# Square sums of the up weights by TensorE in place of ScalarE

## Reference

```python
kv = ctx @ W_k.T + b_k                      # ctx [4, 512, 128]
out = einsum('bij,bjd->bid', layernorm(x), kv)
sim = einsum('bid,bjd->bij', out, kv) * 512 ** -0.5
sim = layernorm(sim) * ln_gamma + ln_beta
x = x + softmax(sim)
n = layernorm(x)
scores = einsum('btd,ed->bte', n, Wg)       # 8 experts, the best 2 per token
w = softmax of the best 2 scores, on their experts, else 0
h = silu(n @ W1[e].T) * (n @ W2[e].T)       # W1, W2 [8, 352, 512]
y = sum over e of w[e] * (h @ W3[e].T)      # W3 [8, 512, 352]
return x + y
```

## Time and profile before

| | us |
|---|---|
| median of 3 runs | 399.23 (399.21 to 400.86) |
| profiled execution | 399.87 |
| its span in the profile | 397.8 |
| around the span | 2.1 |

### The profile page before, as it was taken

One profiled execution on the slowest core, in us unless ns is written; L12 is line 12 of the kernel. 1 busy time (PEld: TensorE's weight loads), 2 busy tenths in 40 slices (PEclk: granted clock), 3 DMA queues, 4 the chain that ended last, 5 costly groups with the idle time before them and its releaser, 6 DMA issues.

```text
span 397.8 us, 8115 instructions
## 1 busy us (share of the span) xinstructions
PE 362.7 (91%) x2277; PEld 239.1 (60%) x2277; DVE 253.2 (64%) x677; ACT 251.1 (63%) x433; POOL 156.7 (39%) x189
## 2 busy tenths in 40 slices
PE   6869799889797699999999999999999999999981
PEld 5445567567784356566666666666666666666640
DVE  1336566987978895763466757667676766757660
ACT  2168787857650698994475666656666575666650
POOL 2114564555831204225544353433435344352321
PEclk9989989996855799999999999999999999999997
DMA  7998799996840214425353545545354453544424
GB/s 224 418 416 322 251 339 356 398 326 230 250 158 2 80 29 64 97 53 87 77 94 67 105 66 98 78 84 95 70 104 68 93 86 75 107 63 100 77 32 53
DMA packets 21833, 57.60 MB, mean 145 GB/s; under 512 B 4832, under 2 KB 4960, under 8 KB 20256
## 3 DMA queue, kind: packets, MB, share of 16 engines
q0 software_dynamic: 8736, 20.53, 29.1%
q1 hardware_dynamic: 11040, 21.62, 15.3%
q10 hardware_dynamic: 2016, 14.94, 10.3%
HBM read 38.17 MB, written 18.91 MB: 143 GB/s over the span
## 4 chain that ended last, share of the span: by engine, by line
PE 63%; DVE 4%; issue 3%; DMA 3%; POOL 1%; ACT 1%; POOLq 1%; ACTq 0%; DVEq 0%
PE bank L1214 35%; PE bank L1235 15%; PE bank L1225 5%; PE bank L1205 4%; PE bank L1257 3%; DMA out<-kvj_s,sidx 1%; DMA ng_s<-n_table,gidx 1%; PE bank L1122 1%; DMA n_table<-wrow 1%; DVE Wp L793 1%; PE bank L1106 1%; DVE stage L817 0%; PE bank L1049 0%; POOLq L73 0%; POOL rstd L418 0%
## 5 line engine op out<-in xcount | busy, mean ns | idle before, releaser
L1214 PE MATMUL bank<-Wp,kvg_s 128*128 x480 | 79.7, 317 | 2.6 <-DVE kvg_s L949 2.4
L1214 PE MATMUL bank<-Wp,kv_s 128*128 x456 | 74.3, 313 | 0.2
L943 DVE SCALAR_TENSOR_TENSOR stage<-W,w3sc,stage 128x512 f16<-128x512 f16 x93 | 66.9, 748 | 7.5 <-ACT stage L615 7.5
L1235 PE MATMUL bank<-stage,n_s 128*128 128x512 f16 (+1 forms) x279 | 65.3, 379 | 1.5 <-issue 1.5
L1214 PEld LDWEIGHTS bank<-Wp,kvg_s 128*128 128x128 f16 x480 | 47.3, 99 | 31.0 <-issue 5.9
L615 ACT ACTIVATE stage<-W,w3sc 128x512 f16 x93 | 63.4, 719 | 0.0
L475 POOL DMA_INDIRECT out<-oT_s,sidx x20 | 31.8, 1589 | 76.8 <-ACT oT_s L646 69.4
L1214 PEld LDWEIGHTS bank<-Wp,kv_s 128*128 128x128 f16 x456 | 44.4, 98 | 26.2 <-issue 3.3
L475 POOL DMA_INDIRECT out<-kvj_s,sidx x19 | 30.1, 1585 | 66.8 <-ACT kvj_s L646 64.3
L459 POOL DMA_INDIRECT ng_s<-n_table,gidx x39 | 39.0, 1000 | 32.1 <-DVE gidx L912 13.8
L970 DVE TENSOR_TENSOR n_s<-bank,n_s 128x384 f16<-128x384 f32 x31 | 17.3, 558 | 51.8 <-ACT n_s L628 51.8
(11 more groups left out here) (188 smaller groups left out, 564.7 us busy)
## 6 DMA issues: line engine op xcount, KB each, us to landing
Wp<-in_w ACTq DMA_DIRECT2D x6, 1408.0 KB, 10.3
W<-in_w ACTq DMA_DIRECT2D x8, 768.0 KB, 5.8
stage<-in_xT SPq DMA_DIRECT2D x4, 1024.0 KB, 7.3
W<-in_x SPq DMA_DIRECT2D x12, 256.0 KB, 7.4
out<-W SPq DMA_DIRECT2D x12, 256.0 KB, 8.4
Wp<-in_w SPq DMA_DIRECT2D x2, 1408.0 KB, 13.4
n_table<-n_s SPq DMA_DIRECT2D x8, 256.0 KB, 3.6
n_table<-x_s SPq DMA_DIRECT2D x8, 256.0 KB, 4.1
```

Source lines behind the costliest of these rows:

```text
L943: eng.scalar_tensor_tensor(w3p[r][:, W3N + c * D:W3N + (c + 1) * D], W3[:, bass.ds(e * W3N + c * D, D)], w3sc[:, bass.ds(e, 1)], w3p[r][:, ...
L1214: mm = eng.matmul(bank[2 * which + r][:, 0:H], n_, w_, start=(c == 0 and k == 0), stop=(c == DC - 1 and k == 2))
L1235: mm = eng.matmul(ybank(t)[:, :], h_, w_, start=(c == 0 and k == 0), stop=(c == HC - 1 and k == 2))
```

## The change

The squares leave ScalarE. TensorE takes the upper 16 bits of each float32 word as a bfloat16 (a view with a step of two elements, 4 bytes), and multiplies each 128x128 block of expert k's weight by itself, transposed: 22 blocks, added up in 128 columns of bank 5. On the diagonal of that product stand the square sums of the 128 column positions. VectorE multiplies it by the identity and sums each row into `wsq` (`diagonal`). The sum over partitions, as before, is over all 128 of them. Only the upper halves of the words are used, so the scale is of slightly truncated weights; the scale is divided out again.

The products take the place of the warm matmuls in slots 0 to 13: all 22 in slots 0 and 1, then 11 a slot. Slot 14 has neither, 15 and 16 keep the warm run. The products of expert k wait for its load and for VectorE's reading of expert k-1's diagonal (`s_wq`). The chain to the scales starts one slot later (15 in place of 14) and so do its steps; on GpSimd the power now stands behind the norm of its slot and not ahead. `table(0)` goes from slot 13 to 14. The issue of the loads is in the same slots.

```diff
@@ -56,6 +56,7 @@
 GROUPS = ((0, 4), (4, 4), (8, 4), (12, 3), (15, 1))
 WARM_GATHER = 12
 WARM_SLOT = 12
+GRAM_SLOTS = ((0,), (1,), (2, 3), (4, 5), (6, 7), (8, 9), (10, 11), (12, 13))
 WARM_START = 48
 NSCALE = 2.0 ** 10
 WSCALE = 2.0 ** 15
@@ -90,7 +91,7 @@
 
         xT_s = stage[:, 0:DC * N]
         ctx_s = stage[:, DC * N:DC * N + T]
-        wjunk = Wp[:, 0:WH].bitcast(BF16)
+        upper = [Wp[:, (e + 1) * 2 * W12N:(e + 2) * 2 * W12N].bitcast(BF16).rearrange("p (n t) -> p n t", t=2)[:, :, 1] for e in range(E)]
         x_s = [W3[:, g * D:(g + 1) * D] if g < G - TPB else stage[:, DC * N + (g - G + TPB) * D:DC * N + (g - G + TPB + 1) * D]
                for g in range(G)]
         wk_s = sb("wk_s", [P, C])
...
@@ -225,8 +227,8 @@
         s_w = [sem(f"s_wl{i}") for i in range(E)]
         s_w3 = [sem(f"s_w3_{i}") for i in range(E)]
 
-        s_wq, s_wqp, s_wsum, s_wmax, s_wrs, s_wsc, s_wrec, s_winv = [
-            sem(n) for n in ("s_wq", "s_wqp", "s_wsum", "s_wmax", "s_wrs", "s_wsc", "s_wrec", "s_winv")]
+        s_wg, s_wq, s_wqp, s_wmax, s_wrs, s_wsc, s_wrec, s_winv = [
+            sem(n) for n in ("s_wg", "s_wq", "s_wqp", "s_wmax", "s_wrs", "s_wsc", "s_wrec", "s_winv")]
         s_hi, s_lo = sem("s_hi"), sem("s_lo")
         s_w3q, s_w3qp, s_w3s, s_w3r, s_w3sc, s_w3rec, s_yinv, s_yt = [
             sem(n) for n in ("s_w3q", "s_w3qp", "s_w3s", "s_w3r", "s_w3sc", "s_w3rec", "s_yinv", "s_yt")]
@@ -431,12 +433,12 @@
                 if real(bn_):
                     scale(bn_, in_)
                 n = TPB * (b + 1) + i - (TPB - 1)
-                if n == 2 * E - 1:
-                    eng.wait_ge(s_wmax, 1)
-                    eng.tensor_tensor(wrs[:, :], wsum[:, :], half[:, 0:1].to_broadcast([P, E]), ALU.pow).then_inc(s_wrs, 1)
                 b1, i1 = lag(b, i, 1)
                 if real(b1):
                     norm(b1, i1)
+                if n == 2 * E:
+                    eng.wait_ge(s_wmax, 1)
+                    eng.tensor_tensor(wrs[:, :], wsum[:, :], half[:, 0:1].to_broadcast([P, E]), ALU.pow).then_inc(s_wrs, 1)
                 if i == 1 and real(b + 1):
                     gamma_keys(b + 1)
                 if n == 17:
@@ -511,7 +513,6 @@
             def slot(b, i):
                 n = TPB * (b + 1) + i - (TPB - 1)
                 weight_loads(n)
-                weights(n)
                 b3, i3 = lag(b, i, 3)
                 if real(b3):
                     g = g_of(b3, i3)
@@ -561,12 +562,6 @@
                 cols = bass.ds(b * TPB, TPB)
                 eng.activation(edl[:, cols], dlt[:, cols], ACT.Exp).then_inc(s_ed, 1)
 
-            def squares(k, h):
-                eng.wait_ge(s_w[k], 16)
-                wait(eng, s_wq, 2 * k + h)
-                eng.activation(wjunk, wst[k][:, h * WH:(h + 1) * WH], ACT.Square,
-                               accum_out=wsq[:, k, h:h + 1]).then_inc(s_wq, 1)
-
             def w12_high(k, h):
 
                 if k >= E:
@@ -589,17 +584,10 @@
                         eng.wait_ge(s_n, (e + 1) * W3N // D)
                     eng.dma_start(W3[:, e * W3N:(e + 1) * W3N], w3[e]).then_inc(s_w3[e], 16)
 
-            def weights(n):
-
-                if n // 2 + 1 < E:
-                    squares(n // 2 + 1, n % 2)
-
             eng.wait_ge(s_key, 16 * 3)
             kv_evac(0)
             kvj_evac(0)
             o_evac(0)
-            squares(0, 0)
-            squares(0, 1)
             batches(slot)
             router_exp(B - 1)
 
@@ -768,9 +756,13 @@
 
             def weight_sums():
                 eng.wait_ge(s_wqp, 1)
-                eng.tensor_reduce(wsum[:, :], bank[7][:, E:3 * E].rearrange("p (e h) -> p e h", h=2), AX.X, ALU.add).then_inc(s_wsum, 1)
-                eng.wait_ge(s_wsum, 1)
-                eng.tensor_tensor(wsum[:, :], wsum[:, :], guard[:, :], ALU.max).then_inc(s_wmax, 1)
+                eng.tensor_tensor(wsum[:, :], bank[7][:, E:2 * E], guard[:, :], ALU.max).then_inc(s_wmax, 1)
+
+            def diagonal(k):
+
+                eng.wait_ge(s_wg, k + 1)
+                eng.tensor_tensor_reduce(diag[:, :], bank[5][:, P:2 * P], ident[:, :], 1.0, 0.0, ALU.mult, ALU.add,
+                                         wsq[:, k:k + 1]).then_inc(s_wq, 1)
 
             def weight_scale():
 
@@ -805,6 +797,10 @@
                     hold(eng, 4, (s_T, g + 1), (s_E, g - 1))
                     eng.tensor_tensor_reduce(L_s[:, k, :], L_s[:, k, :], beta_s[:, :], 1.0, 3.0e38, ALU.add, ALU.min,
                                              lmin[:, k:k + 1]).then_inc(s_L, 1)
+                n = TPB * (b + 1) + i - (TPB - 1)
+                for k in range(E):
+                    if n == GRAM_SLOTS[k][-1] + 1:
+                        diagonal(k)
                 b1, i1 = lag(b, i, 1)
                 if real(b1):
 
@@ -822,8 +818,7 @@
                     square_in(b + 1)
                 if i == 2 and real(b + 1):
                     gram_copy(b + 1)
-                n = TPB * (b + 1) + i - (TPB - 1)
-                if n == 2 * E:
+                if n == 2 * E + 1:
                     weight_scale()
                 if i == 0 and real(b - 2):
                     router_weights(b - 2)
@@ -853,7 +848,7 @@
                     scale_in(bn_, in_)
                 if i == 3 and real(b + 2):
                     centre_keys(b + 2)
-                if n == 2 * E - 2:
+                if n == 2 * E - 1:
                     weight_sums()
                 if i == 0 and 1 < b < B:
                     places(b - 2)
@@ -1108,8 +1103,18 @@
 
             def weight_norms(n):
                 wait(eng, s_sc, n - 4)
-                eng.wait_ge(s_wq, 2 * E)
-                eng.matmul(bank[7][:, E:3 * E], ones[:, :], wsq[:, :, :].rearrange("p e h -> p (e h)"), start=True, stop=True).then_inc(s_wqp, 1)
+                eng.wait_ge(s_wq, E)
+                eng.matmul(bank[7][:, E:2 * E], ones[:, :], wsq[:, :], start=True, stop=True).then_inc(s_wqp, 1)
+
+            def weight_gram(k, first, last):
+
+                eng.wait_ge(s_w[k], 16)
+                wait(eng, s_wq, k)
+                for c in range(first, last):
+                    w_ = upper[k][:, c * P:(c + 1) * P]
+                    mm = eng.matmul(bank[5][:, P:2 * P], w_, w_, start=(c == 0), stop=(c == W12N // P - 1))
+                if last == W12N // P:
+                    mm.then_inc(s_wg, 1)
 
             def router(b, i):
                 g = g_of(b, i)
@@ -1166,7 +1171,12 @@
                     keys(b + 2)
                 if i == 0 and real(b + 1):
                     turn_keys(b + 1)
-                warm(ones16[:, :], WARM_SLOT)
+                if n > GRAM_SLOTS[E - 1][-1] + 1:
+                    warm(ones16[:, :], WARM_SLOT)
+                for k, slots in enumerate(GRAM_SLOTS):
+                    if n in slots:
+                        h, part = slots.index(n), W12N // P // len(slots)
+                        weight_gram(k, h * part, (h + 1) * part)
                 turn_n(*lag(b, i, 2))
                 if i == 1 and real(b + 1):
                     gram(b + 1)
@@ -1174,7 +1184,8 @@
                 if i == 2 and real(b + 1):
                     gram_outs(b + 1)
                     sims(ba, ia)
-                if n == 13:
+                if n == 14:
+                    eng.wait_ge(s_wq, E)
                     table(0)
             eng.wait_ge(s_const, NCONST)
             warm(ones16[:, :], WARM_START)
```

More of the change, by code:

```diff
@@ L129, in build @@
         guard = sb("guard", [P, E])
-        wsq = sb("wsq", [P, E, 2])
+        wsq = sb("wsq", [P, E])
+        diag = sb("diag", [P, P])
         wsum = sb("wsum", [P, E])
```

## The result

| | before | changed kernel |
|---|---|---|
| median of the runs, us | 399.86 (399.21 to 400.86, 4 runs) | 403.94 (402.52 to 404.42, 4 runs) |
| profiled execution, us | 399.87 | 402.52 |
| its span, us | 397.8 | 399.9 |
| ratio to before (95% interval) | | 1.0087 (1.0062 to 1.0112) |

The change made the kernel slower by about 4 us, where no change was forecast, and the median lies beyond the upper end of the range (402.2). The profiled execution is the fastest of its four: its trace shows a little less of the loss than the median has. The ratios leave out runs in a slower state, one of `a4_three` (482.15 us) and two of `b2_no_squares_loads` (402.75 and 403.21); the medians have them in.

The account below looks back on a forecast made before the run. With the expert stage fixed, the time hung on when the first gathered rows reach TensorE. Terms -2.4 -0.9 +0.9 +1.1 +1.2 = -0.1 us took 399.23 to 399.1 us; terms' ends 397.2 to 401.2, range with rivals 396.0 to 402.2.

Parts of the forecast that it names:

- The hand-over in slot 10: Slot 10: TensorE's products wait for VectorE's diagonal behind the minimum, making outs(3) late; +1.1 us.
- Part 1: Slots 0 to 3: squares off ScalarE let the scaling start sooner; 2.4 us gained, from 0.7 to 3.1.
- the unfavourable end: Start, slots 0 to 3: earlier third-weight load shares the engines, xT lands at 32.1, gain only 0.7 us.
- rival D: Start: ScalarE's freed time only issues loads earlier, which hold up inputs; gain 0.7 us, 400.8 us, chance 0.11.
- Part 2: Slots 4 to 16: squares are hidden by waits and gain nothing, except 0.9 us in slot 13.
- The 0.9 us of slot 13: Slot 13: a square delays the router's exp, for which VectorE idles; removing it gains 0.9 us.
- Rival A: Slots 5, 6, 7, 10, 11: ScalarE paces, so removed squares pass through by half; 3.7 us faster, 395.5 us, chance 0.24.
- Part 3: TensorE, slots 0 to 14: products replace warm matmuls, 4-byte step costs nothing; taken as 0, bound 0.6 us per eleven.
- Rival B: TensorE, slots 0, 1, 2, 7, 10: strided products run at half rate; 3.0 us slower, 402.1 us, chance 0.11.
- Part 4: VectorE's diagonals cost 0.9 us in slots 8, 12, 14; TensorE's wait for one in slot 10 costs 1.1 us.
- Rival C: Slots 1, 2, 6 too: TensorE waits for the diagonal, VectorE for products; 401.6 us, chance 0.14.
- Part 5: Slots 16 and 17: pow behind GpSimd's norm delays VectorE's weight_scale and router copy; +1.2 us, from 0.5 to 2.0.

Follow-up runs that it names:

- a4_three: Changed kernel with third and fourth loads held, diagonals of experts 2 to 7 at the slot's head, pow ahead of the norm: 398.77 us, 0.9968.
- b2_no_squares_loads: Kernel before without ScalarE's squares, nothing in their place, third and fourth up-weight loads held until the first two landed: 398.42 us, 0.9947.
- the last two kernels: Changed kernel with only slot 10's diagonal at its slot's head, 400.80 us, and with only those of experts 2, 3, 4, 6, 7 there, 403.96 us.
- a2_diag_first: Changed kernel with VectorE's diagonals of experts 2 to 7 at the head of their slots: 401.08 us, 1.0022.
- a6_two: Changed kernel with two edits, third and fourth loads held and diagonals of experts 2 to 7 at the slot's head: 399.17 us, 0.9964.
- a0_after: The changed kernel itself, unaltered, in a second set of five runs: 403.32 us, 1.0070.

## Why the prediction was wrong, step by step

Two terms of the sum failed. The start was put at -2.4 us on the ground that alpha of tile 3 would be last at slot 4; xT was, and the lead there was 1.3 us. The hand-over in slot 10 was put at +1.1 us, the delay of one arrival; TensorE's rows there have 3.4 us, because the wait came together with a lower clock. The late norms, +1.2, were put too high and hid some of it.

**Part 1, the start: the step that failed first.** The mechanism of both sides was written down and the wrong side was taken. The scaling of tile 0 came at 22.59 (22.3 forecast). But xT, and not alpha of tile 3, was last at slot 4: it landed at 33.03 (16.97 + 16.06), even later than the 32.1 of the unfavourable end, and the lead at tile 3 was 1.3 us, nearer to the 0.7 of rival D than to the 2.4 taken. My estimate had the second and the third weight share evenly from 19.3 on and counted only the rows' mean rate. I also gave the late xT no price beyond its lateness. In the changed kernel's trace it had none (clock 1.00), but in the kernel without squares the clock fell in the idle time ahead of `outs(1)`, and there the late load cost 4.0 us. No row of before could show that amount, but the earlier trace rows beside the earlier trace rows (1.49 against 0.83 us for the same twelve matmuls) could have named it as a possible price of each wait on TensorE. So rival D held, and its own number, 400.8, was too low, because the hand-over's step was too small as well.

The Trainium skill (DMA: Bandwidth & Descriptors, section Queues, rings and completion order) says that an engine takes packets in turn from the queues that have work; by that rule xT would land near 32. It landed at 33.0 and, with the loads held, after 12.3 us. The trace agrees with the direction and shows, in the changed kernel, somewhat more than the rule gave; the order of the packets is in no row.

**Part 2, squares of slots 4 to 16.** Right that they are hidden: with nothing in their place and the loads held, all squares together, those of the start included, are worth 2.1 us. The 0.9 us of slot 13 can't be seen by itself in any run. Rival A, ScalarE paces (395.5), falls with the same run: 398.4.

**Part 3, TensorE.** Right. Eleven products take 0.80 us at full clock and 22 take 1.42, no more than warm matmuls; a step of 4 bytes costs nothing. Rival B falls. The Trainium skill (SBUF — State Buffer, section Door 1: The DMA port swizzle) had it so, and these rows agree.

**Part 4, the hand-over: right place, wrong size.** The diagonal takes 0.29 us with 0.08 for the accumulator's read. The 0.9 us for three of them on the path can't be told from nothing: the two edits' kernel, which has products, diagonals and late norms all in, stands about 0.7 us above the kernel with nothing in place of the squares (0.9964 against 0.9947, with intervals that overlap), where the prediction has 0.9 + 1.2. Slot 10 was forecast at 1.1 us and is 2 to 3 (3.2 between the last two kernels, 1.9 to 2.6 from `a2_diag_first`): the wait of 1.25 us (1.2 forecast) is only part, and beside it TensorE ran the products, the transposes, `gram` and a part of `outs(3)` at the lower clock. That the place of one 0.29 us operation is worth about 3 us is shown by the last two kernels. That the rest is the lower clock is shown by the rows of TensorE, from one execution of each kernel; what starts the fall is open. Rival C, the same wait in every pair, falls: moving the five other diagonals gave nothing.

**Part 5, the late norms: mis-sized.** The wait on VectorE came as forecast, in the changed kernel too, and the router copy behind it was late as forecast:

```profile
111.87 1.65 POOL L441 TENSOR_TENSOR wrs<-wsum,half 128x8 f32<-128x8 f32 x1
...
113.55 0.17 DVE L770 TENSOR_SCALAR wscale<-wrs 128x8 f32<-128x8 f32 x1 [2.09 <-POOL wrs L441]
...
115.25 0.17 DVE L834 COPY sc<-bank 128x8 f32<-128x8 f32 x1
```

But that copy is only 1.7 us later than before (113.51), and 1.3 of these were there already at the scaling of tile 15. The kernel before with the same chain moved by itself shows the step's own size. Its pow took 1.65 us and not 2.00 and was done at 112.36, not 112.9, and the work behind it was a little shorter than taken, so that the copy came at 114.09 and not at 114.75: 0.6 us later than before, where 1.2 was forecast. The first gather then came 0.5 us later (128.04 against 127.54), so the claim that from 113.5 on VectorE has no pause until the table is done held: the copy is 14.0 us ahead of the gather in all three traces. The time rose by 0.2 us (-0.6 to 1.0). GpSimd's own order is no way out, since to exchange its two steps gave nothing.

**The sum by what was measured**, from the ratios: squares off, loads held: -2.1. Products, diagonals and late norms in their place: +0.7, which makes the -1.4 of `a6_two`. Both edits undone: +4.2, of which the loads are 1.6 to 2.5 and slot 10 1.9 to 3.2, which makes the +2.8 of `a0_after`. No change was forecast and a loss came because two terms, -2.4 and +1.1, were each taken from an arrival time alone; the first also took the wrong arrival.

The prediction's own range was added up wrongly, too. Its terms' ends, with the fixed -0.9, give -2.6 to +3.4 us, that is 396.6 to 402.6 from the median of 399.23, and not 397.2 to 401.2. The measured median lies above that as well.

The version with both edits, 0.9964 (0.9945 to 0.9984), is 1.4 us faster than the kernel before, of the 2.1 us that leaving the squares out altogether gives in this order of work.

## What to carry to other kernels

When work is taken off an engine that also issues DMAs, its later issues move forward with it: list them, and where they share the DMA engines with a load that is waited for, tie them to what they were behind. When a result is handed from one engine's slot to another's, put the short producer at the head of its slot; one diagonal of 0.29 us in the wrong place was worth about 3 us. And price a new wait of TensorE twice, once as the wait and once with the matmuls behind it at half clock: here waits of 1.0 to 1.6 us in slot 10 came with the lower clock in every trace, and one of 2.48 us ahead of `outs(1)` without it.

## What the runs showed of the hardware

Less work made a kernel slower: without 22 us of squares, 402.41 against 399.99 us, by a load that landed later and, in its trace, matmuls that ran at the lower clock (6.15 us for eight, 3.70 at full clock). A load of 1024 KB that shares the engines with a load issued at the same moment took 14.7 to 16.4 us, and 11.9 to 13.4 us (once 15.0) where the other was held back. TensorE's clock fell between 70 and 74 us in eleven of the sixteen profiled kernels: in some while it was busy with the scores of similarity or the matmuls behind them, in others during the wait for the diagonal, and it stayed down for 3.4 or 6.8 us. In the changed kernel TensorE had not stood idle for more than 1.18 us at a time in the 10 us ahead of the fall. Why it falls in some kernels and not in others stays open.
